# Three stacked attention passes with a routed expert layer: phase two's routing arithmetic on VectorE rewritten, phase three's indirect gathers issued in other slots

## The chip, the cores and the metric

The program runs on one core of one Trainium2 chip. The metric is device time in microseconds from launch to end. A core has five engines that run side by side and meet only at semaphores: TensorE (PE), VectorE (DVE), ScalarE (ACT), GpSimd (POOL) and SyncE (SP), whose queue here only issues transfers.

## The reference

```python
# x: 16 sequences x 256 tokens x 128 features, float32
x = x + layernorm(attention(layernorm(x)))                    # 16 heads, causal
f = layernorm(x)
f = f + attn(ln(f)); f = f + token_moe(ln(f))                 # top 2 of 8 experts, per token
f = f + attn(ln(f)); f = f + seq_moe(ln(f))                   # top 2 of 8, per sequence
x = x + layernorm(f)
...
def _combine_weights(logits):
    vals, idx = jax.lax.top_k(logits, K)
    w = jax.nn.softmax(vals, axis=-1)
    onehot = (idx[..., None] == jnp.arange(E)).astype(w.dtype)
    return jnp.sum(w[..., None] * onehot, axis=-2)
```

## The kernel before

An item is one sequence (256 tokens, two tiles of 128) in one of three attention passes; 16 items make phase one, the next 16 phase two, the last 16 phase three. All queues are written out by hand as a software pipeline. One **step** advances the pipeline by one item and has four **slots**, k = 0 to 3, one for each group of four heads. In step n every engine works on items n-4 to n+2: score maxima of item n, exponentials and values a slot or three behind, the output projection and residual of item n-2, normalisation of item n+2.

The order on each engine is the text of `pe_slot`, `act_slot`, `dve_slot` and `pool_slot`; nothing is reordered, so whatever waits on an engine holds up all that stands behind it there. Landmarks in a step:

- `pe_qk` (L375) opens a step on PE, so its start times count the steps. The maxima (L307, L315) go to one of two PSUM banks, and the next maxima into a bank wait until `dve_reduce` (L616, DVE) has read it. `dve_split_max` (L625) closes a slot's maxima, and `pe_max_T` (L359) waits for it. `pe_o2` (L400) waits for `dve_norm` (L635).
- POOL masks the exponentials (`pool_select`, L902, two a slot), splits q and k into terms (L911, L917), and issues all indirect transfers.

Routing in phase two, for one item: `dve_logits` (L719); `dve_top` piece 0 (top 8 of 8, L731), piece 1 (their indices L736, and the difference of the two best logits, L738, into `gap_all`), piece 2 (L742); a step later `dve_place` piece 0 (one-hots, L754), piece 1 (the sum of the two one-hots, L762, for `pe_rank`, L431 to L435), piece 2 (L765, L769), piece 3 (one-hots times places, two instructions at L773), pieces 4 and 5 (L778, L782). Then `pool_send` scatters the item's rows to DRAM with four indirect transfers (L927).

Between phases two and three the pipeline drains. `dve_tables` turns the counts into tables of jobs in 26 dependent instructions: 18 that the jobs wait for, 8 that phase three needs, the last 3 of them with the exponential of `gap_all` that `act_gap` (L1112) makes. 72 expert jobs of 128 rows follow, their rows loaded from DRAM (L1364, first transposed by PE at L1278), their outputs stored to `y_routed`.

In phase three `pool_fetch` gathers an item's expert outputs with four indirect transfers, pieces 0 to 3 (L946); piece 0 is preceded by a copy of the addresses (L943), whose end POOL waits for. `dve_combine` (L797) adds them: rank 0 in slot 0 once all four have landed, rank 1 in slot 1. The buffer `y_got` is double, by the item's parity. Item n+2 is combined in step n; its four pieces are issued in slots 0 to 3 of step n-1. The last stage, 32 expert passes for the sequence experts, is untouched.

Of the kernel before, what the change touches and what calls it, by code (L numbers as in the profile page):

```python
# [7 lines left out]
ALU = mybir.AluOpType  # L8
# [25 lines left out]
STACK_DMAS = TERMS  # L34
NTOP, NPLACE = 6, 7

# [8 lines left out]
def build(nc, x_in, w_qk, w_v, w_o, b_qk, b_v, b_o, ln1, ln2, gate_w, gate_b, e_w1, e_b1, e_w2, e_b2, out):  # L45
# [13 lines left out]
    with ExitStack() as ctx:  # L59
        def sb(name, shape, dt=F32):  # L60
            return ctx.enter_context(nc.sbuf_tensor(name, shape, dt))
# [86 lines left out]
        lgt = sb("lgt", [P, 2, E])  # L148
        mx = sb("mx", [P, 2, 8])
        mi = sb("mi", [P, 2, 8], U32)  # L150
# [78 lines left out]
        def item(step, d):  # L229
            n, par, phase, lo, hi = step  # L230
            if isinstance(n, int):
                v = n + d
                return Item(v, v % 2, v // B) if lo <= v < hi else None
            return Item(n + d, (par + d) % 2, phase)
# [487 lines left out]
        def dve_top(i, piece):  # L722

            u = i.v - B
            at = NTOP * u
            if piece == 0:
                dve.wait_ge(lg_sb, u + 1)
                need(dve, top, at)
                alone(dve)
                for j in range(2):  # L730
                    nc.vector.max(out=mx[:, j], in_=lgt[:, j]).then_inc(top, 1)  # L731
            elif piece == 1:
                dve.wait_ge(top, at + 2)
                alone(dve)
                for j in range(2):
                    nc.vector.max_index(out=mi[:, j], in_max=mx[:, j], in_values=lgt[:, j]).then_inc(top, 1)  # L736
                gap = gap_all[:, bass.ds(2 * i.b, 2)]
                nc.vector.tensor_tensor(gap, mx[:, :, 1], mx[:, :, 0], ALU.subtract).then_inc(top, 1)  # L738
            else:
                dve.wait_ge(top, at + 4)  # L740
                alone(dve)
                nc.vector.tensor_copy(expert_all[:, bass.ds(2 * i.b, 2)], mi[:, :, 0:TOP]).then_inc(top, 1)  # L742

        def dve_place(i, piece):
# [14 lines left out]
            elif piece == 1:  # L759
                dve.wait_ge(placed, at + 1)  # L760
                need(dve, rank_ps, u)
                nc.vector.tensor_tensor(either[:], onehot[:, :, 0], onehot[:, :, 1], ALU.add).then_inc(placed, 1)  # L762
            elif piece == 2:
# [6 lines left out]
            elif piece == 3:  # L770
                dve.wait_ge(placed, at + 4)
                for t in range(2):
                    m = nc.vector.tensor_tensor(picked[:, t], onehot[:, t],  # L773
                                                places[:, t:t + 1].to_broadcast([P, TOP, E]), ALU.mult)
                m.then_inc(placed, 1)
            elif piece == 4:
# [181 lines left out]
        def pool_slot(step, k):  # L958
# [21 lines left out]
            if k == 3 and nxt and nxt.phase == 2:  # L980
                pool_bias(nxt)
            nxt3 = item(step, 3) if step_phase(step) == 2 else None
            if nxt3:
                pool_fetch(nxt3, k)
            sending = first if k == 3 else item(step, -5)
# [54 lines left out]
        EARLY = [(0, B - 2), (B - 2, B)]  # L1040
        NTABLE_JOBS, NTABLE = 18, 26


        def dve_tables():
# [9 lines left out]
            def view(shape):  # L1054
# [37 lines left out]
                                                op0=ALU.mult, op1=ALU.add))  # L1092
            assert n[0] == NTABLE_JOBS

            t = view([P, NT * TOP, E])
# [14 lines left out]
        def act_gap():  # L1110
            act.wait_ge(top, NTOP * B)
            nc.scalar.activation(gap_all[:], gap_all[:], ACT.Exp).then_inc(gate_a, 1)  # L1112
# [465 lines left out]
        def _(_):  # L1578
# [25 lines left out]

            run_steps(act, behind(act_slot, 0, [loaded, *others]), *RUNS[0])
            act_gap()
            act.wait_ge(table, NTABLE_JOBS)
            pads(act, range(E // 2, E))
            act_jobs()
            act.wait_ge(w1_got, JOBS)  # L1610
# [99 lines left out]
```

## Time and profile before

| | |
|---|---|
| median of three runs | 1174.61 us (1172.34 to 1177.23) |
| profiled execution | 1179.62 us |
| its span | 1177.6 us, mean granted clock 0.961 of full speed |
| PE busy | 1025.1 us, 87% |
| DVE busy | 920.7 us, 78% |
| ACT busy | 780.4 us, 66% |
| POOL busy | 701.0 us, 60% |

Shares of the span mix stages with different limits. By the starts of L375, phases one and two fill the span from 18.7 to about 530 us, the drain and the tables lie between about 530 and 590, the jobs between 590 and 735, phase three between 735 and about 1006, and the sequence experts after it. In a timeline row the columns are start and duration in us, engine, line, operation, output and inputs, shapes and count; the bracket is the idle time of the engine before it and what ended that idle time. A duration begins when the instruction does, so neighbours can overlap and an instruction that waits for a memory port shows the wait in its duration.

### The profile page before, as it was taken

To read this page: it belongs to the slowest core of one execution; us is meant where nothing else is said; L and a number is where in the kernel's file an instruction comes from. 1 tells how busy PE (TensorE), PEld (TensorE's weight loads), DVE (VectorE), ACT (ScalarE), POOL (GpSimd) and SP (SyncE) were. 2 spreads that over 40 slices of the span, in tenths; PEclk is the share of its full clock that TensorE was granted. 3 is DMA by queue.
4 is the path that set the end of the run, shared out by engine and by line. 5 is a ranking of instruction groups with operands and counts; after the bars stand their busy time and mean duration, and the time that the engine had idled before them with its cause. 6 is when DMAs were issued, how large, how long until landed. Compare 5 with 4: busy or idle time off the path is not lost. (4 is left out here: it accounts for less than half of the span.)

```text
span 1177.6 us, 34922 instructions
## 1 busy us (share of the span) xinstructions
PE 1025.1 (87%) x10453; PEld 796.5 (68%) x10453; DVE 920.7 (78%) x2712; ACT 780.4 (66%) x1908; POOL 701.0 (60%) x1034
## 2 busy tenths in 40 slices
PE   1799999999999999998199998288898998989996
PEld 0567676676676766665199998166666665768986
DVE  4679999999989999997647665378898888856675
ACT  1577777777787777775078886167677776755564
POOL 3356666666667888886623332677787786533332
PEclk9999999999999999999589999699999999989999
DMA  5343122221212222221122222244222222100000
GB/s 147 101 113 83 51 56 54 53 56 52 54 51 61 65 66 65 64 68 34 54 62 69 66 70 74 65 126 124 70 63 65 59 65 53 48 2 15 19 19 22
DMA packets 120406, 73.71 MB, mean 63 GB/s; under 512 B 10688, under 2 KB 115264, under 8 KB 120256
## 3 DMA queue, kind: packets, MB, share of 16 engines
q1 hardware_dynamic: 101600, 53.12, 16.5%
q10 hardware_dynamic: 14560, 10.35, 3.2%
q0 software_dynamic: 4096, 8.40, 2.5%
q8 instruction: 76, 1.25, 0.5%
q14 instruction: 74, 0.61, 0.2%
HBM read 21.68 MB, written 11.60 MB: 28 GB/s over the span
## 5 line engine op out<-in xcount | busy, mean ns | idle before, releaser
L616 DVE TENSOR_REDUCE wide<-bank 128x2 f32<-128x512 f32 (+1 forms) x576 | 388.7, 678 | 55.4 <-PE bank L307 40.4
L503 ACT ACTIVATE prob<-bank 128x512 f32<-128x512 f32 x576 | 337.4, 592 | 89.2 <-PE bank L329 58.9
L902 POOL TENSOR_SCALAR_AFFINE_SELECT prob<-prob 128x512 f32<-128x512 f32 x384 | 249.9, 657 | 105.3 <-ACT prob L503 103.4
L348 PE MATMUL bank<-prob,vaug 128*32 128x256 f32 (+1 forms) x3072 | 166.9, 335 | 5.7 <-ACT oT L509 3.2
L1237 POOL COPY w_job<-w_s 128x512 f32 x104 | 67.9, 654 | 154.6 <-PE bank L1206 153.6
L315 PE MATMUL bank<-stack 126*128 126x256 bf16 x768 | 149.8, 276 | 0.0
L334 PE MATMUL bank<-stack 128*128 128x256 bf16 x768 | 148.4, 274 | 1.4 <-ACT prob L503 1.4
L1228 ACT ACTIVATE prob<-bank,b_job 128x128 f32<-128x128 f32 (+1 forms) x416 | 132.5, 400 | 23.7 <-PE bank L1206 12.3
L1217 PE MATMUL bank<-w_job,prob 128*128 128x128 f32 x1088 | 139.7, 276 | 1.9 <-issue 1.8
L348 PEld LDWEIGHTS bank<-prob,vaug 128*32 128x32 f32 x3072 | 81.7, 110 | 80.3 <-issue 48.4
L1217 PEld LDWEIGHTS bank<-w_job,prob 128*128 128x128 f32 x1088 | 132.1, 192 | 4.9 <-issue 3.6
L311 PE MATMUL bank<-maskneg,identb 128*128 128x256 bf16 x384 | 106.6, 278 | 5.5 <-DVE wide L616 4.5
L514 ACT COPY mT<-bank 8x256 bf16<-8x256 bf16 x192 | 68.2, 355 | 45.4 <-PE bank L359 43.3
L329 PE MATMUL bank<-stack 128*128 128x128 bf16 x768 | 75.2, 220 | 15.7 <-DMA stack<-mT 15.1
L927 POOL DMA_INDIRECT x_routed<-hk,x_at x64 | 64.9, 1015 | 37.8 <-DVE x_at L782 18.7
L334 PEld LDWEIGHTS bank<-stack 128*128 128x128 bf16 x768 | 73.9, 98 | 14.3 <-ACT prob L503 3.1
L315 PEld LDWEIGHTS bank<-stack 126*128 126x128 bf16 x768 | 76.5, 100 | 7.0 <-issue 0.5
L625 DVE TENSOR_TENSOR wide<-wide 128x8 bf16<-128x8 f32 x192 | 74.1, 386 | 6.6
L1206 PE MATMUL bank<-oT,w_job 128*128 128x128 f32 x576 | 77.8, 279 | 0.0
L946 POOL DMA_INDIRECT y_got<-y_routed,y_at x64 | 64.4, 1007 | 22.3 <-issue 8.7
L305 PE MATMUL bank<-maskneg,identb 128*128 128x512 bf16 x192 | 74.0, 386 | 4.2 <-DMA stack<-parts 2.2
L307 PEld LDWEIGHTS bank<-stack 126*128 126x128 bf16 x768 | 60.0, 98 | 24.8 <-issue 1.1
(183 smaller groups left out, 2073.1 us busy)
## 6 DMA issues: line engine op xcount, KB each, us to landing
stack<-parts SPq DMA_DIRECT2D x576, 64.0 KB
w_s<-e_w ACTq DMA_DIRECT2D x32, 256.0 KB, 3.0
oT<-x_routed SPq DMA_DIRECT2D x72, 64.0 KB, 1.8
y_routed<-oT SPq DMA_DIRECT2D x36, 128.0 KB, 1.9
stack<-mT SPq DMA_DIRECT2D x192, 4.0 KB
out<-x_all SPq DMA_DIRECT2D x16, 128.0 KB, 1.8
b_all<-e_b ACTq DMA_DIRECT2D x2, 512.0 KB, 8.3
x_routed<-hk,x_at POOLq DMA_INDIRECT x64
```

Of the source, the lines that this page charges most:

```text
L311: nc.tensor.matmul(o[:, :, P:T], identb[:], maskneg[:, 0:2], start=True, stop=False, skip_group_check=True)
L315: m = nc.tensor.matmul(o[:, h], q[:, hh, P:T], k[:, hh, :], start=False, stop=True, skip_group_check=True)
L329: m = nc.tensor.matmul(bk[:, h * P:(h + 1) * P], k[:, p0 + h, P:T], q[:, p0 + h, P:T], start=True, stop=True)
L334: m = nc.tensor.matmul(bk[:, h * T:(h + 1) * T], k[:, hh, 0:P], q[:, hh, :], start=True, stop=True)
L348: m = nc.tensor.matmul(o, w, (prob0, prob1)[kb][:, g % 2, h], start=kb == 0, stop=kb == 1, skip_group_check=True)
L503: nc.scalar.activation(o, s, ACT.Exp, scale=SCALE).then_inc(exp_done, 1)
L616: nc.vector.tensor_reduce(o, s, AX.X, ALU.max, negate=True).then_inc(max_done, 1)
L625: nc.vector.tensor_tensor(upper(g)[:, :, 0], negm[:, g % 2, :, 1], upper(g)[:, :, 1], ALU.subtract).then_inc(negmax, 1)
L902: nc.gpsimd.affine_select(out=t, in_=t, compare_op=ALU.is_ge, fill=0.0, base=0, pattern=[[0, HG], [1, P]], channel_multiplier=-1).then_inc ...
L1206: m = nc.tensor.matmul(bank[2 * par + c // 2][:, (c % 2) * T:(c % 2) * T + width], w1_job[:, par, c * P:(c + 1) * P], rows, start=True, st ...
L1217: m = nc.tensor.matmul(y_bank[par][:, t * P:(t + 1) * P], hid[:, par, c, t * P:(t + 1) * P], w2_job[:, par, c], start=(c == 0), stop=(c == ...
L1228: nc.scalar.activation(hid[:, par, c, 0:width], bank[2 * par + c // 2][:, (c % 2) * T:(c % 2) * T + width], ACT.Gelu, bias=b1_job[:, par, ...
```

## The change

1. The logits' difference (L738) leaves the per-item routing. The top-8 values go to `mx_all`, kept for all tiles, and one instruction in `dve_tables`, the 19th of now 27, takes all differences. `act_gap` waits for it, and moves on ACT from ahead of the four pad transfers to behind them.
2. The two one-hots are joined by a `tensor_reduce` with maximum over the rank axis in place of a `tensor_tensor` addition.
3. One product for both tiles (128x32) in place of two (128x16).
4. In phase three the gathers move. Pieces 0 and 1 of an item go to slot 3 of the step before the one that held them, piece 2 to slot 0, piece 3 to slot 2; slot 1 issues none. The first step issues pieces 0 to 2 of the first item together.

```diff
-NTOP, NPLACE = 6, 7
+NTOP, NPLACE = 5, 7
...
-        mx = sb("mx", [P, 2, 8])
+        mx_all = sb("mx_all", [P, NT, 8])
...
+            mx = mx_all[:, bass.ds(2 * i.b, 2)]
...
-                gap = gap_all[:, bass.ds(2 * i.b, 2)]
-                nc.vector.tensor_tensor(gap, mx[:, :, 1], mx[:, :, 0], ALU.subtract).then_inc(top, 1)
...
-                nc.vector.tensor_tensor(either[:], onehot[:, :, 0], onehot[:, :, 1], ALU.add).then_inc(placed, 1)
+                nc.vector.tensor_reduce(either[:], onehot[:].rearrange("p t r e -> p t e r"), AX.X, ALU.max)\
+                  .then_inc(placed, 1)
...
-                for t in range(2):
-                    m = nc.vector.tensor_tensor(picked[:, t], onehot[:, t],
-                                                places[:, t:t + 1].to_broadcast([P, TOP, E]), ALU.mult)
-                m.then_inc(placed, 1)
+                nc.vector.tensor_tensor(picked[:], onehot[:], places[:].unsqueeze(2).to_broadcast([P, 2, TOP, E]),
+                                        ALU.mult).then_inc(placed, 1)
...
-            nxt3 = item(step, 3) if step_phase(step) == 2 else None
-            if nxt3:
-                pool_fetch(nxt3, k)
+            if step_phase(step) == 2:
+                d, pieces = {0: (3, (2,)), 1: (3, ()), 2: (3, (3,)), 3: (4, (0, 1))}[k]
+                if step[0] == step[3] - 3 and d == 3:
+                    pieces = range(pieces[-1] + 1) if k == 0 else pieces
+                for n in pieces:
+                    if item(step, d):
+                        pool_fetch(item(step, d), n)
...
+            step(nc.vector.tensor_tensor(gap_all[:], mx_all[:, :, 1], mx_all[:, :, 0], ALU.subtract))
...
         def act_gap():
-            act.wait_ge(top, NTOP * B)
+            act.wait_ge(table, NTABLE_JOBS + 1)
...
-            act_gap()
             act.wait_ge(table, NTABLE_JOBS)
             pads(act, range(E // 2, E))
+            act_gap()
```

## Rows read from the trace of the kernel before

**Rows 1.** Windows; busy us of PE, PEld, DVE, ACT, POOL, PEclk, DMA share, GB/s

```profile
350.00:500.00 150.00, 141.79 (x1616) 104.14 (x1614) 143.42 (x455) 113.51 (x259) 120.40 (x166) 1.00 0.24 64
750.00:950.00 200.00, 170.15 (x1823) 119.30 (x1822) 164.31 (x403) 134.51 (x310) 154.94 (x217) 0.96 0.31 84
```

**Rows 2.** Timeline of PE: the first instruction of some steps (L375)

```profile
252.10 1.08 PE L375 MATMUL bank<-xT,wqk_s 128*128 128x256 f32 x4
...
283.12 1.08 PE L375 MATMUL bank<-xT,wqk_s 128*128 128x256 f32 x4
...
346.12 1.08 PE L375 MATMUL bank<-xT,wqk_s 128*128 128x256 f32 x4
...
361.93 1.08 PE L375 MATMUL bank<-xT,wqk_s 128*128 128x256 f32 x4
...
514.42 1.08 PE L375 MATMUL bank<-xT,wqk_s 128*128 128x256 f32 x4
...
758.93 1.89 PE L375 MATMUL bank<-xT,wqk_s 128*128 128x256 f32 x4
...
881.66 1.08 PE L375 MATMUL bank<-xT,wqk_s 128*128 128x256 f32 x4
...
898.63 1.13 PE L375 MATMUL bank<-xT,wqk_s 128*128 128x256 f32 x4
...
1006.41 1.08 PE L375 MATMUL bank<-xT,wqk_s 128*128 128x256 f32 x4
```

**Rows 3.** Timeline of DVE in one step of phase two

```profile
395.12 0.46 DVE L738 TENSOR_TENSOR gap_all<-mx 128x2 f32<-128x2 f32 x1
395.50 0.68 DVE L616 TENSOR_REDUCE wide<-bank 128x2 f32<-128x512 f32 x1
...
399.80 0.61 DVE L762 TENSOR_TENSOR either<-onehot 128x16 bf16<-128x16 f32 x1
400.84 0.69 DVE L616 TENSOR_REDUCE wide<-bank 128x4 f32<-128x512 f32 x1 [0.43 <-PE bank L307]
...
401.90 1.14 DVE L679 TENSOR_TENSOR f_all<-f_all,att 128x256 f32<-128x256 f32 x1
...
410.70 0.56 DVE L773 TENSOR_TENSOR picked<-onehot,places 128x16 f32<-128x16 f32 x2
```

**Rows 4.** Instructions by tile; ns min/median/max, first and last start

```profile
L754 DVE TENSOR_TENSOR onehot<-expert_all,iota_e x16: 181/669/677, 348.3 to 569.6; 128x32 f32<-128x32 f32 x16
L762 DVE TENSOR_TENSOR either<-onehot x16: 160/612/614, 349.3 to 569.8; 128x16 bf16<-128x16 f32 x16
...
L778 DVE TENSOR_REDUCE place_all<-picked x16: 178/180/186, 362.3 to 571.1; 128x4 f32<-128x32 f32 x16
```

**Rows 5.** Timeline of PE in the same step of phase two: two waits for DVE

```profile
397.95 0.44 PE L400 MATMUL bank<-ident,on 128*128 128x128 f32 x2 [0.35 <-DVE on L635]
...
404.89 0.29 PE L359 MATMUL bank<-identb,wide 128*128 128x128 bf16 x2 [0.28 <-DVE wide L625]
```

**Rows 6.** Timeline of DVE and PE where the jobs begin

```profile
587.80 0.22 DVE L1245 COPY b_job<-b_all 128x128 f32 x1
...
590.29 0.45 PE L1278 MATMUL bank<-ident,oT 128*128 128x128 f32 x1 [19.94 <-DMA oT<-x_routed]
```

**Rows 7.** Who waited for the gathers (L946): us, times

```profile
  DVE f_all L797: 30.2, 16
```

**Rows 8.** Timeline of POOL, DVE and PE around one combine of phase three

```profile
842.24 1.11 POOL L946 DMA_INDIRECT y_got<-y_routed,y_at  x1 [0.17 <-issue]
...
845.44 0.98 POOL L946 DMA_INDIRECT y_got<-y_routed,y_at  x1 [0.16 <-issue]
...
849.21 0.61 DVE L797 SCALAR_TENSOR_TENSOR f_all<-y_got,weight_all,f_all 128x128 f32<-128x128 f32 x2 [2.42 <-DMA y_got<-y_routed,y_at]
...
849.83 0.97 POOL L946 DMA_INDIRECT y_got<-y_routed,y_at  x1 [0.82 <-ACT prob L503]
...
852.12 0.27 PE L359 MATMUL bank<-identb,wide 128*128 128x128 bf16 x2 [2.98 <-issue]
```

More of the change, by code:

```diff
@@ L1040, in build @@
         EARLY = [(0, B - 2), (B - 2, B)]
-        NTABLE_JOBS, NTABLE = 18, 26
+        NTABLE_JOBS, NTABLE = 18, 27
         def dve_tables():
```

## The prediction

> **What bounds the kernel now.** I read the windows by stage first, because the change touches two stages that need not have the same limit. In phase two PE is busy 141.79 of 150 us and DVE 143.42 at the full clock: both are nearly full, and DVE is the fuller one. In phase three PE is busy 170.15 and DVE 164.31 of 200, so neither is full and something makes both wait; the granted clock there averages 0.96 [rows 1]. The starts of L375 on PE then give the length of a step. Phase one: (283.12 - 252.10) / 2 = 15.51 us. Phase two, once all of the routing and the scatters run: (514.42 - 361.93) / 9 = 16.94; the one step in which the routing's DVE work is already there but the scatters are not, 346.12 to 361.93, takes 15.81. Phase three: (1006.41 - 758.93) / 14 = 17.68, while a step in it that goes well, 881.66 to 898.63, takes 16.97 [rows 2]. The waits say why. In phase two PE waits 0.35 us at L400 and 0.28 at L359 for DVE [rows 5]. In phase three DVE waits for the gathers in all 16 items, 30.2 us together [rows 7], and in the worst steps PE then stands still for 2.98 us at L359, for which DVE should have finished its maxima [rows 8].
>
> **Phase two: the difference, L738, removed.** It starts at 395.12 and the next instruction at 395.50: it costs DVE 0.38 us a step, in a stretch with no idle time, ahead of the normalisation that L400 waits for [rows 3]. All of this is worth having.
>
> **The two products made one.** The pair takes 0.56 us [rows 3]. The trace has no 128x32 product, but L754 has that shape, two inputs in SBUF and one result: 0.181 at its shortest, 0.669 in the median [rows 4]. So the new instruction saves between 0.56 - 0.18 = 0.38 and nothing. The first of the old pair passes quickly and the second is held, which speaks for the low price; I take 0.2 us saved. This too lies ahead of L400.
>
> **The one-hots joined by a maximum.** The addition takes 0.612 in the median and 0.160 at its shortest; a reduction of as many inputs, L778, takes 0.178 to 0.186 in all its 16 executions [rows 4]. So DVE gains 0.61 - 0.18 = 0.43. But right behind it DVE already idles 0.43 us until PE's L307 [rows 3], so this gain only lengthens that idle time, and I count nothing; at worst (a result as slow as the old one) it costs nothing either.
> L762 is 0.61 or 0.16 with the same shape, while L778 never varies. The Trainium skill (SBUF — State Buffer, Who interferes with whom) says that a `tensor_tensor` with both inputs in SBUF contends with a GpSimd instruction that reads SBUF, and that a `tensor_reduce` on trn2 never does; the trace agrees. By that rule L762 becomes 0.18. A sentence of the same page (SBUF: two separate sides) speaks against it: reads that go to a new 16-byte line each time pay a penalty, and the new reduction steps 32 bytes between its two inputs; no run here shows that penalty. By neither does the sum move, since the idle time behind takes both.
>
> **What DVE's relief is worth.** DVE saves 0.38 + 0.2 = 0.58 us a step on the loop through L400. PE can give back no more than the difference to the step that ran undisturbed, 16.94 - 15.81 = 1.13, and no less than its wait of 0.35 at L400 [rows 2, 5]. The 0.28 at L359 comes after L679, which takes 1.14 us [rows 3] and is untouched; it stays unless POOL's work happens to shift. I take 0.57 us: the 0.35 and a little over a quarter of the other 0.78, in waits too small to have rows. Nine full steps are measured and two more run before the drain: 11 x 0.57 = 6.3 us, with ends 9 x 0.35 = 3.2 and 11 x 1.13 = 12.4.
>
> **The tables.** One more dependent instruction, about 0.2 us (the shortest two-input ones, rows 4), stands behind the 18 that the jobs wait for. DVE's preparations end at 587.80 + 0.22 = 588.02 and PE's first job instruction starts at 590.29, waiting for a load that comes from instruction 18 by way of SP [rows 6]. So 2.27 us cover it: nothing; without cover 0.2 us. `act_gap` moves behind four transfers on ACT's queue; its reader is DVE's instruction 25, and what it is late by, up to 2 us, has the same cover. What is queued behind it on ACT waits for the same load as PE. Nothing again.
>
> **Phase three: the gathers moved.** POOL still issues four gathers and one copy per item; SP's queue is not touched. Take the worst step. Piece 3 is issued at 845.44 and takes POOL 0.98; DVE starts its combine at 849.21, so the landing takes 849.21 - 846.42 = 2.79 us after that. DVE was ready at 849.21 - 2.42 = 846.79 [rows 8]. In the new order the last piece goes where piece 2 stood, 842.24 to 843.35; with the same 2.79 it lands at 846.14, still 0.65 before DVE is ready. On average DVE waits 30.2 / 16 = 1.9 us [rows 7], so the usual case has more room. The wait goes in every step. The new first pieces are a whole step ahead of their combine and need the item two before it to be combined, which happened two slots earlier on DVE.
> What remains is a step without this stall. It can't be shorter than phase one's 15.51, which has about the same matmuls on PE; and 881.66 to 898.63 shows 16.97 where PE did not wait for the combine in slot 0, with all other waits still in it. The order itself helps those: the copy of addresses and the 0.82 us that POOL waits behind it [rows 8] leave slot 0, where they stood ahead of the q/k split. On the other side DVE's second combine in slot 1 still meets POOL's masks. I take the middle, (15.51 + 16.97) / 2 = 16.24: 14 x (17.68 - 16.24) = 20.2 us. Ends: 14 x 0.71 = 9.9 and 14 x 2.17 = 30.4. The first step of the phase issues the same pieces in nearly the same order: about nothing.
>
> **Sum.** 6.3 + 20.2 = 26.5 us. From the profiled execution's 1179.62: 1153.1. That execution lies 5.0 above the median of the runs, 1174.61, so for the median I say 1148.
>
> **Rivals.**
> *Only the stall goes.* Steps of phase three fall to 16.97 because DVE and POOL go on blocking each other at L797 and the masks, and phase two gives only the wait at L400: 9.9 + 3.2 = 13.1, 1161.5. For it: in phase three DVE and POOL are both above 77% busy [rows 1] and that step was measured. Against it: POOL's slot 0 gets lighter. Chance 0.20.
> *Both stages reach their floors.* 12.4 + 30.4 = 42.8, 1132. It needs L679 to meet POOL in another phase and no contention at all. Chance 0.08.
> *The stall is the transfer's, not the issue's.* If landing were held by something that ends at a fixed point of the step, earlier issue would not help; only phase two's 6.3 would remain: 1168.3. Against it: landing after issue varies, but the worst is 2.79 us. Chance 0.04.
> *POOL piles up in slot 3: slower.* Ahead of slot 0's first mask stood one gather, 0.16 + 0.98 = 1.14 us; now stand a copy of about 0.2, 0.82 of waiting, and two gathers of 0.97 with 0.16 between: 3.1. The masks of slot 0 come 2.0 us later, and the values (L348) on PE need them in slot 1. Against it: POOL is busy 154.94 of 200 us [rows 1], so about 4 us of each step are waits that can take it up. If all 2.0 were uncovered it would cost 28 us and more than undo the 26.5: 1176 as it stands, and over 1180.5 if the masks are 2.4 us late. It decides from 1.9 us uncovered. Chance 0.05, of which 0.03 beyond 0.5%.
>
> **How the numbers follow.** The forecast has 0.63. 0.5% of 1174.6 is 5.9 us, about what a measurement of this kernel can tell from no change. Faster by more (below 1168.7): 0.63 + 0.20 + 0.08 + half of the transfer rival, 0.92. Within: 0.05. Slower: 0.03. The range reaches from 1136 (a good part of the way to the floors) to 1162 (only the stall goes); what lies outside is the extreme of the floors and the last two rivals, and the outer parts of the second.
>
> **What the new profile would show.** L946 no longer releases DVE: its wait at L797 falls from 30.2 us to near nothing, but for the first item. Steps of phase three by L375: 16.0 to 16.5, with few waits of PE over 1 us at L359. L762 a reduction of 0.18; L738 once, at the tables. Steps of phase two: 16.3 to 16.5, with no wait at L400 and a longer idle time of DVE before L307. First job instruction on PE as far behind the drain as before. I am wrong if the masks of slot 0 (L902) now hold L348, or if steps in phase three stay at 17 because L311 waits for DVE behind the second combine.

## The result and the profile after

The changed kernel takes 1156.79 us in the median of 4 runs (1155.36 to 1158.09), the kernel before 1173.79 on the same chip. The ratio is 0.9851, with a 95% interval of 0.9824 to 0.9877: 17.0 us faster. The forecast was 1148 with a range of 1136 to 1162, so the sign and the range held, and the gain is 9 us short of the point.

First the windows over the two stretches of [rows 1].

```profile
350.00:500.00 150.00, 140.44 (x1629) 105.66 (x1650) 138.91 (x442) 113.20 (x262) 121.66 (x169) 1.00 0.24 65
750.00:950.00 200.00, 179.51 (x1966) 130.26 (x1994) 170.45 (x434) 143.42 (x334) 164.17 (x233) 0.97 0.32 88
```

In phase two PE is as busy as before (140.44 of 150 us against 141.79) while DVE has fallen by 4.5 us: there DVE got lighter, and PE went hardly faster. In phase three every engine does more in the same 200 us, at nearly the same clock (0.97 against 0.96): waits have gone. The starts of L375 on PE, as in [rows 2], say how much:

```profile
344.12 1.08 PE L375 MATMUL bank<-xT,wqk_s 128*128 128x256 f32 x4
...
359.93 1.08 PE L375 MATMUL bank<-xT,wqk_s 128*128 128x256 f32 x4
...
510.53 1.08 PE L375 MATMUL bank<-xT,wqk_s 128*128 128x256 f32 x4
...
754.36 1.17 PE L375 MATMUL bank<-xT,wqk_s 128*128 128x256 f32 x2
...
837.69 1.08 PE L375 MATMUL bank<-xT,wqk_s 128*128 128x256 f32 x4
...
853.89 1.08 PE L375 MATMUL bank<-xT,wqk_s 128*128 128x256 f32 x4
...
984.36 0.87 PE L375 MATMUL bank<-xT,wqk_s 128*128 128x256 f32 x3
```

The step without scatters takes 359.93 - 344.12 = 15.81 us, to the hundredth what it took before. A full step of phase two takes (510.53 - 359.93) / 9 = 16.73 (before 16.94). A step of phase three takes (984.36 - 754.36) / 14 = 16.43 (before 17.68), and the usual one 853.89 - 837.69 = 16.20. The spans, 1156.4 against 1177.6, differ by 21.2 us: 14 steps of phase three give 17.5, nine of phase two 1.9, and the way from 510.53 to the first job 2.3. Another 2.0 stem from ahead of 346.12, in code that the change doesn't touch; the jobs, the start of phase three and the tail took 1.1, 0.6 and 0.9 more.

Who waited for the gathers (L944), as in [rows 7]:

```profile
  DVE f_all L795: 12.9, 2
```

It is 12.9 us in two waits, where it was 30.2 in 16. Both belong to the first two items (10.69 us at the first, 2.25 at the second). The timeline of DVE shows the first of them, and one of the later combines, which have no wait:

```profile
736.13 1.32 DVE L795 SCALAR_TENSOR_TENSOR f_all<-y_got,weight_all,f_all 128x128 f32<-128x128 f32 x4 [10.69 <-DMA y_got<-y_routed,y_at]
...
839.86 0.62 DVE L795 SCALAR_TENSOR_TENSOR f_all<-y_got,weight_all,f_all 128x128 f32<-128x128 f32 x2
```

The first two items waited nearly as long in the kernel before:

```profile
741.65 1.31 DVE L797 SCALAR_TENSOR_TENSOR f_all<-y_got,weight_all,f_all 128x128 f32<-128x128 f32 x4 [9.93 <-DMA y_got<-y_routed,y_at]
...
749.50 1.26 DVE L797 SCALAR_TENSOR_TENSOR f_all<-y_got,weight_all,f_all 128x128 f32<-128x128 f32 x4 [3.59 <-DMA y_got<-y_routed,y_at]
```

So 13.5 of the 30.2 us were no part of the steady steps. The other 14 items waited 0.51 to 2.42 us, 16.7 together, and it is these waits that went.

The new instructions by tile, as in [rows 4] (ns: shortest, median, longest; first and last start):

```profile
L761 DVE TENSOR_REDUCE either<-onehot x16: 175/188/190, 347.3 to 564.3; 128x16 bf16<-128x32 f32 x16
L772 DVE TENSOR_TENSOR picked<-onehot,places x16: 173/486/522, 357.7 to 565.3; 128x32 f32<-128x32 f32 x16
```

The maximum never takes over 0.19 us, as foreseen. The single product takes 0.49 in the median, hardly less than the pair's 0.56.

### The profile page after: what moved, and what is told of

It reads as the page before. It is cut to its first block, busy times and chain, and to the rows that moved or that the text cites. A ratio compares the mean times of both kernels' runs of the same rounds, so it can differ in the third digit from the quotient of the medians.

```text
span 1156.4 us, 34796 instructions
## 1 busy us (share of the span) xinstructions
PE 1007.1 (87%) x10358; PEld 794.4 (69%) x10453; DVE 891.7 (77%) x2681; ACT 772.8 (67%) x1908; POOL 695.3 (60%) x1034
## 4 chain that ended last, share of the span: by engine, by line
PE 31%; DVE 5%; issue 5%; DMA 3%; POOL 3%; ACT 2%; SPq 1%; POOLq 0%; DVEq 0%; ACTq 0%
PE bank L1220 10%; PE bank L1209 10%; PE bank L348 2%; DMA stack<-mT 2%; DVE wide L616 2%; PE bank L393 1%; POOL y_got L944 1%; PE bank L315 1%; PE bank L334 1%; PE bank L375 1%; PE bank L311 1%; PE bank L1281 1%; DVE f_all L795 1%; PE bank L329 1%; PE bank L381 1%
## 5 line engine op out<-in xcount | busy, mean ns | idle before, releaser
L348 PE MATMUL bank<-prob,vaug 128*32 128x256 f32 (+1 forms) x3072 | 165.6, 333 | 7.5 <-issue 3.8
L1240 POOL COPY w_job<-w_s 128x512 f32 x104 | 64.3, 619 | 158.3 <-PE bank L1209 157.1
L348 PEld LDWEIGHTS bank<-prob,vaug 128*32 128x32 f32 x3072 | 81.5, 109 | 81.4 <-issue 49.4
L307 PE MATMUL bank<-stack 126*128 126x128 bf16 x768 | 75.0, 219 | 15.7 <-ACT prob L503 6.4
L944 POOL DMA_INDIRECT y_got<-y_routed,y_at x64 | 63.9, 998 | 24.7 <-POOL y_at L941 13.1
L625 DVE TENSOR_TENSOR wide<-wide 128x8 bf16<-128x8 f32 x192 | 69.8, 364 | 6.6
```

What stands on the lines that cost most here:

```text
L307: m = nc.tensor.matmul(o[:, h], q[:, p0 + h, 0:P], k[:, p0 + h, 0:P], start=False, stop=True, skip_group_check=True)
L348: m = nc.tensor.matmul(o, w, (prob0, prob1)[kb][:, g % 2, h], start=kb == 0, stop=kb == 1, skip_group_check=True)
```

## Where phase two's gain went

The same step of phase two in the timelines, first of the kernel before, three lines of PE, ACT and POOL that were not among the rows ahead of the prediction; its next L375 follows at 412.79:

```profile
395.85 1.08 PE L375 MATMUL bank<-xT,wqk_s 128*128 128x256 f32 x4
...
398.97 0.60 ACT L503 ACTIVATE prob<-bank 128x512 f32<-128x512 f32 x1
...
401.59 1.17 POOL L911 TENSOR_TENSOR rest<-qkf,parts 128x512 f32<-128x512 f32 x1
```

And after the change, lines of PE, ACT, POOL and DVE from the step that starts at 393.40:

```profile
395.01 0.44 PE L400 MATMUL bank<-ident,on 128*128 128x128 f32 x2
...
396.35 0.58 ACT L503 ACTIVATE prob<-bank 128x512 f32<-128x512 f32 x1
...
397.88 1.00 POOL L925 DMA_INDIRECT x_routed<-hk,x_at  x1 [0.16 <-issue]
...
397.90 0.69 DVE L616 TENSOR_REDUCE wide<-bank 128x4 f32<-128x512 f32 x1 [0.86 <-PE bank L307]
...
398.92 1.17 POOL L909 TENSOR_TENSOR rest<-qkf,parts 128x512 f32<-128x512 f32 x1
...
398.96 1.42 DVE L679 TENSOR_TENSOR f_all<-f_all,att 128x256 f32<-128x256 f32 x1
```

By "held" this text means that a DVE instruction takes longer than at its shortest while a GpSimd instruction runs beside it; L679 at its shortest takes 0.42 us, in the step from 344.12 for one. The "split" is GpSimd's first subtraction of the q/k terms, L911 before and L909 after. Count from the start of the step. L400 stands at 1.61 instead of 2.10, with no wait: PE is 0.49 us earlier, and DVE idles 0.86 before the reduction instead of 0.43. So far all is as forecast. But ScalarE's exponential starts at 2.95 instead of 3.12, only 0.17 earlier, since it stands behind ScalarE's own queue. GpSimd's mask, scatter and q/k split follow it in order, and the split starts at 5.52 instead of 5.74. L679 on DVE started earlier, but is held until after the split has ended: 1.42 us instead of 1.14. It ends at 6.98 instead of 7.19. The step got shorter by exactly this 0.21.

Over all nine steps from 359.93 the rest of the step, from the end of L679 on, takes 9.75 us (9.74 to 9.76), and in the kernel before as well (9.75, once 9.79). In these steps the length is L679's end plus a constant. It is not so in the step from 344.12, which has no scatters: there L679 ends at 5.89 and 9.92 follows, so with an end as early as that something else sets the step. The experiments test the constant below.

## Experiments

**The two halves apart.** First the kernel before with only the new order of the gathers:

```
-            nxt3 = item(step, 3) if step_phase(step) == 2 else None
-            if nxt3:
-                pool_fetch(nxt3, k)
+            if step_phase(step) == 2:
+                d, pieces = {0: (3, (2,)), 1: (3, ()), 2: (3, (3,)), 3: (4, (0, 1))}[k]
...
```

> The kernel before with the gathers of phase three moved and the routing as it was. If the gain is mostly the stall at the combine, steps of phase three fall from 17.68 to about 16.4 us as in the changed kernel, steps of phase two stay at 16.94, and the time is about 1160 to 1161 us (a ratio to before of 0.989). If instead the gathers' order gives little and the routing most, it stays above 1168 (0.995).

Measured: 1160.09 us, ratio 0.9851 (0.9809 to 0.9893). Steps of phase three take 16.37, those of phase two 16.93. The waits for the gathers in its trace:

```profile
  DVE f_all L797: 12.4, 2
```

Then the changed kernel with the old order of the gathers (the same lines the other way round).

> The changed kernel with the gathers back in slots 0 to 3. Phase two's steps as in the changed kernel, 16.73 us, phase three's as before. Theory: 2 us in the steps and 2 in the drain, so 1169 to 1171 us (0.996 to 0.998). Rival, the routing is worth the 6.3 us that I had forecast: 1167.5 or less (0.9946). The two edits should add up to the whole within 2 us.

Measured: 1175.55 us, ratio 0.9982 (0.9959 to 1.0005). Steps of phase two take 16.74, those of phase three 17.59, with two of about 20 us (20.41 and 19.70) as in the kernel before (19.75 and 20.26). The waits for the gathers:

```profile
  DVE f_all L795: 30.9, 15
```

What follows: the new order of the gathers alone gives the whole of what the run times can show, and without it the stall is there as before. The routing by itself can't be told from no change by run times: its interval reaches from 4.8 us faster to 0.6 slower. Its 0.2 us a step is read from the step lengths.

**The routing's three edits, one at a time.** Each was taken back in the changed kernel. The difference once per item:

```
                     nc.vector.max_index(out=mi[:, j], in_max=mx[:, j], in_values=lgt[:, j]).then_inc(top, 1)
+                gap = gap_all[:, bass.ds(2 * i.b, 2)]
+                nc.vector.tensor_tensor(gap, mx[:, :, 1], mx[:, :, 0], ALU.subtract).then_inc(top, 1)
...
-            step(nc.vector.tensor_tensor(gap_all[:], mx_all[:, :, 1], mx_all[:, :, 0], ALU.subtract))
...
-            act.wait_ge(table, NTABLE_JOBS + 1)
+            act.wait_ge(top, NTOP * B)
```

> The changed kernel with the logits' difference back in each item, its maximum and its one product kept. Read by steps of phase two. If this difference (0.38 us of VectorE ahead of L400) is what shortened the step, steps go back from 16.73 to about 16.9, the wait of PE at L400 comes back, about 0.3 us. If the other two edits carry it, steps stay at 16.73 to 16.75.

Measured: one run at 1160.57; steps of phase two 16.90 (six of nine between 16.90 and 16.92). Its step from 394.46, timelines of PE and DVE:

```profile
396.53 0.44 PE L400 MATMUL bank<-ident,on 128*128 128x128 f32 x2 [0.33 <-DVE on L635]
...
400.49 1.13 DVE L679 TENSOR_TENSOR f_all<-f_all,att 128x256 f32<-128x256 f32 x1
```

L400 waits 0.33 us again, the split is back at 5.69, L679 ends at 7.16 and the step is 16.90: of the 0.21 the difference carries 0.17.

The addition in place of the maximum:

```
-                nc.vector.tensor_reduce(either[:], onehot[:].rearrange("p t r e -> p t e r"), AX.X, ALU.max)\
-                  .then_inc(placed, 1)
+                nc.vector.tensor_tensor(either[:], onehot[:, :, 0], onehot[:, :, 1], ALU.add).then_inc(placed, 1)
```

> The changed kernel with the addition in place of the maximum. VectorE idles 0.86 us behind the maximum, so the 0.43 us that the addition costs more should only shorten that: steps of phase two stay at 16.73 us, the idle time before L616 falls to about 0.43. Rival, it lay on the path: steps of 17.0 or more.

Measured: one run at 1156.06; steps of phase two 16.73. By tile, its addition:

```profile
L761 DVE TENSOR_TENSOR either<-onehot x16: 162/172/611, 347.4 to 564.5; 128x16 bf16<-128x16 f32 x16
```

Once the rest had moved, the same addition that took 0.61 before took 0.17: in its step from 393.56 it starts at 397.01, between two masks of GpSimd (396.19 to 396.83 and from 397.25), while in the kernel before it started at 399.80 beside a mask from 399.73 to 400.38. The duration belonged to the place, not to the operation.

The two products in place of one:

```
-                nc.vector.tensor_tensor(picked[:], onehot[:], places[:].unsqueeze(2).to_broadcast([P, 2, TOP, E]),
-                                        ALU.mult).then_inc(placed, 1)
+                for t in range(2):
+                    m = nc.vector.tensor_tensor(picked[:, t], onehot[:, t],
+                                                places[:, t:t + 1].to_broadcast([P, TOP, E]), ALU.mult)
+                m.then_inc(placed, 1)
```

> The changed kernel with the two products of 128x16. Forecast of the prediction: 0.2 us of VectorE. The new single product took 0.49 us where the pair took 0.56, so it should be about 0.07 us and steps stay at 16.73 to 16.80.

Measured: one run at 1157.63; steps of phase two 16.73. The pair takes 0.55 us again and L679 1.36 instead of 1.42: it starts 0.06 later and ends at the same 6.98.

**L679 one place later on DVE.** This is the first attempt to get past the hold: the residual sum behind the next reduction of maxima.

```
-            if i.phase > 0:
-                dve.wait_ge(res, base + 1)
+
+        def dve_residual_sum(i):
+            if i.phase == 1:
+                dve.wait_ge(res, NRES * i.v + 1)
                 nc.vector.tensor_tensor(pair(f_all, i), pair(f_all, i), att[:, i.par], ALU.add).then_inc(res, 1)
...
+                dve_residual_sum(older)
                 dve_residual_stats(older)
```

> The changed kernel with the residual's second addition (L679) put behind the next reduction of maxima in phase two. Moving the scatter showed that L679 is held by whichever GpSimd instruction lies beside it. Port theory: here it meets only the last 0.6 us of the split, the reductions of slot 1 come 0.4 to 1.3 us earlier, PE's wait at L359 in slot 2 (0.27) goes, and steps of phase two fall from 16.73 to about 16.3: 4 to 5 us less than the changed kernel. Rival, the values or the scatter on GpSimd bound the step: it stays at 16.7.

Measured: 1156.25 us, ratio 0.9844 (0.9809 to 0.9878); steps of phase two 16.67. The expected 16.3 did not come. Its step from 393.15, DVE and PE:

```profile
399.25 0.88 DVE L681 TENSOR_TENSOR f_all<-f_all,att 128x256 f32<-128x256 f32 x1
...
401.92 0.28 PE L359 MATMUL bank<-identb,wide 128*128 128x128 bf16 x2 [0.62 <-DVE wide L625]
```

The sum now takes 0.88, but it still ends at 399.25 + 0.88 - 393.15 = 6.98, with the split; the 0.28 us that PE waited at L359 became 0.62. A later place for the held instruction gives only 0.06 us a step (9.69 instead of 9.75 behind its end), since the split ends when it did.

**The scatter of slot 0 moved.** So the split itself has to come earlier. Ahead of it stands slot 0's scatter. Three places for it were tried. The first was slot 1:

```
-                pool_send(sending, (k + 1) % NG)
+                for n in {3: (0,), 0: (), 1: (1, 2), 2: (3,)}[k]:
+                    pool_send(sending, n)
```

> The changed kernel with phase two's scatter of slot 0 issued in slot 1, behind the split of q and k, so that slot 1 issues two and slot 0 none. Port theory: GpSimd's first split (L909) then runs about 1.0 us earlier in the step, is over before the residual's second addition (L679) comes, L679 falls from 1.42 to about 0.45 us, a step of phase two from 16.73 to 15.8 to 16.0 us, and the time by 8 to 10 us to about 1148. Rival, ScalarE's exponential holds PE at L307 (the trace charges 0.54 us a step to it): L679 may get shorter but steps stay at 16.7 and the time at 1157.

Measured: 1162.82 us, ratio 0.9875 (0.9839 to 0.9911); steps of phase two 17.13. The expectation of 15.8 to 16.0 was wrong. Its step from 392.27, POOL and DVE:

```profile
396.73 1.16 POOL L909 TENSOR_TENSOR rest<-qkf,parts 128x512 f32<-128x512 f32 x1
...
398.04 0.85 DVE L679 TENSOR_TENSOR f_all<-f_all,att 128x256 f32<-128x256 f32 x1
...
404.64 0.91 DVE L662 TENSOR_SCALAR hn<-f_all,post_mv,post_r 128x128 f32<-128x128 f32 x2 [0.63 <-POOL post_r L893]
```

The split came at 4.46 and L679 ended at 6.62, 0.36 earlier (held by GpSimd's mask behind the split). But the second scatter in slot 1 pushed back the standard deviations that GpSimd computes behind it, and DVE then waited for them for 0.63 us: the part behind L679 grew from 9.75 to 10.55.

Slot 2 was tried together with another order of the gathers (one a slot, pieces 0, 1, 2, 3 in slots 3, 0, 1, 2):

```
-                pool_send(sending, (k + 1) % NG)
+                for n in {3: (0,), 0: (), 1: (1,), 2: (2, 3)}[k]:
+                    pool_send(sending, n)
...
-                d, pieces = {0: (3, (2,)), 1: (3, ()), 2: (3, (3,)), 3: (4, (0, 1))}[k]
...
+                d, pieces = {0: (3, (1,)), 1: (3, (2,)), 2: (3, (3,)), 3: (4, (0,))}[k]
...
```

> Again one edit in each phase. Phase two: the scatters as 1, 0, 1, 2 alone, the addition where it was. It should meet slot 1's first mask (0.64 us) instead of the split (1.17): L679 about 0.85 us, steps 16.4 to 16.6. Phase three: the gathers one a slot, each one slot earlier than before the change (piece 0 in slot 3, 1, 2, 3 in slots 0, 1, 2), copy kept. If only the landing of the last piece matters, the wait at the combine is gone here too and steps are 16.2 to 16.4, as in the changed kernel; if the free slot 1 matters as well, they stay near 16.9, the length of the steps before that did not stall.

Measured: 1162.04 us, ratio 0.9881 (0.9854 to 0.9908); steps of phase two 17.08, of phase three 16.55. In phase two, DVE and PE:

```profile
399.64 0.42 DVE L679 TENSOR_TENSOR f_all<-f_all,att 128x256 f32<-128x256 f32 x1
...
411.41 0.92 PE L375 MATMUL bank<-xT,wqk_s 128*128 128x256 f32 x3 [1.27 <-ACT xT L602]
```

Here L679 is not held at all: 0.42 us. Yet PE waits 1.27 at the start of the next step, for the transposed input that ScalarE brings late, and the part behind L679 takes 11.35 in this step and 11.07 in the usual one. Phase three has no wait for gathers from the third item on (12.0 us, twice), and its steps are still 0.12 longer than the changed kernel's. Two effects nearly cancel in that tenth: in the usual step the split starts at 5.50 instead of 5.76 to 5.80, but the gather in slot 1 stands behind it, and from the end of GpSimd's second subtraction, L915, to the next L375 it is 7.50 us instead of 7.10.

The third place was slot 3, behind piece 0, where GpSimd waits anyway:

```
-                pool_send(sending, (k + 1) % NG)
+                for n in {3: (0, 1), 0: (), 1: (2,), 2: (3,)}[k]:
+                    pool_send(sending, n)
```

> The changed kernel with slot 0's scatter (piece 1) issued in slot 3 of the step before, right behind piece 0; nothing else differs. It takes the scatter away from ahead of the q/k split L909 without burdening slots 1 and 2, where a second scatter cost 0.4 us a step. In the changed kernel's step from 393.40 the first scatter starts at 394.69 and takes 0.97, the copy 0.40 and the two masks 0.64 and 0.63, then comes the scatter of 1.00 and the split. With both scatters in front (1.26 us more, with the 0.30 between two issues) the masks run at 397.3 and 397.9 and the split starts at 398.6 instead of 398.92. Theory (the end of the split holds L679, and L679 sets the rest of phase two's step): L679 is released 0.3 us earlier, the step falls by 0.2 to 0.3 to 16.45 to 16.55, 11 steps give 2 to 3 us. Rival (GpSimd's masks in order behind the scatters set the pace, whatever L679 takes): the first mask of slot 0 comes 1.26 us later and slot 1's values wait for it; the step lengthens to 17.0 to 17.2, as in the two kernels that had two scatters in one slot. Phase three 16.2 to 16.5 by both.

Measured: 1155.38 us, ratio 0.9818 (0.9784 to 0.9852). Steps of phase two take 16.44, as the theory said. Two of its steps, by PE, POOL and DVE:

```profile
395.30 0.87 PE L375 MATMUL bank<-xT,wqk_s 128*128 128x256 f32 x3
...
400.04 1.15 POOL L909 TENSOR_TENSOR rest<-qkf,parts 128x512 f32<-128x512 f32 x1
...
400.77 1.30 DVE L679 TENSOR_TENSOR f_all<-f_all,att 128x256 f32<-128x256 f32 x1
...
401.16 0.63 POOL L900 TENSOR_SCALAR_AFFINE_SELECT prob<-prob 128x512 f32<-128x512 f32 x1
...
461.38 1.08 PE L375 MATMUL bank<-xT,wqk_s 128*128 128x256 f32 x4
...
466.13 1.16 POOL L909 TENSOR_TENSOR rest<-qkf,parts 128x512 f32<-128x512 f32 x1
...
466.85 0.72 DVE L679 TENSOR_TENSOR f_all<-f_all,att 128x256 f32<-128x256 f32 x1
...
467.25 0.83 POOL L900 TENSOR_SCALAR_AFFINE_SELECT prob<-prob 128x512 f32<-128x512 f32 x1
...
477.32 1.08 PE L375 MATMUL bank<-xT,wqk_s 128*128 128x256 f32 x4
```

In both the split starts 4.74 or 4.75 behind the step's start and L679 at 5.47, and in both GpSimd's mask comes right behind the split. In the first the mask takes 0.63 us and L679 is held on until 0.28 behind the mask, 6.77; the step is 16.52. In the second L679 is free 0.28 behind the split, at 6.19, and it is the mask that takes longer, 0.83; the step is 15.94. Four steps go the first way and this one the second; what decides is not shown. In two more, from 477.32 and 493.64, the split starts later, at 5.14, yet L679 ends at 6.58 and 6.57, and the step is 16.32. So the step follows L679's end, and neither the start of the split nor the end of the mask (6.49, 6.70 and 7.07). The rest behind L679 is 9.74 to 9.76 in eight of the nine steps. It is the same in the kernel before, in the changed one and in all seven experiments that leave L679 in its place and put no second scatter in slot 1 or 2 (this one included), all but for one step in each of three, from an end at 6.19 to one at 7.24.

**The gathers' addresses without the copy.** The new order leaves a copy of the addresses on GpSimd and a wait of 0.82 us for it. Here the gathers read the whole table:

```
-                nc.gpsimd.tensor_copy(y_at[:, i.par], y_at_all[:, bass.ds(2 * i.b, 2)]).then_inc(fetch_at, 1)
-                pool.wait_ge(fetch_at, u + 1)
-                alone(pool)
...
-                bass.IndirectOffsetOnAxis(ap=y_at[:, i.par, t, rank:rank + 1], axis=0))\
+                bass.IndirectOffsetOnAxis(ap=y_at_all[:, 2 * i.b + t, rank:rank + 1], axis=0))\
```

> The changed kernel with the gathers' addresses read straight from the table for all tiles, without the copy and the 0.81 us that GpSimd waits behind it. If GpSimd is what is late in phase three (the masks of slot 0 end at the moment when the split of the maxima wants the port, and the mask of slot 1 holds the values for 0.32 us), its work ends 1.0 us earlier, the waits of PE at L348 (0.32) and at L359 (0.15) go, and steps fall from 16.20 to about 15.8: 5 to 6 us, about 1151. If phase three is held by PE and the transfers of mT, nothing over 1 us is gained.

Measured: 1157.01 us, ratio 0.9821 (0.9785 to 0.9858); steps of phase three 16.44, not the expected 15.8. Its step from 852.67, POOL and DVE:

```profile
854.84 1.25 DVE L795 SCALAR_TENSOR_TENSOR f_all<-y_got,weight_all,f_all 128x128 f32<-128x128 f32 x2
...
856.94 0.63 POOL L900 TENSOR_SCALAR_AFFINE_SELECT prob<-prob 128x512 f32<-128x512 f32 x1 [1.00 <-ACT prob L503]
```

GpSimd was early and then waited 1.00 us for ScalarE's exponential, while its first mask (855.28, 0.66 us) now stood beside DVE's combine, which took 1.25 us instead of 0.62. The split started at 6.02 instead of 5.78.

**All of it together.** Scatters as in the kernel with two in slot 2, L679 later, no copy, and three gathers in slot 3:

```
-                d, pieces = {0: (3, (2,)), 1: (3, ()), 2: (3, (3,)), 3: (4, (0, 1))}[k]
...
+                d, pieces = {0: (3, ()), 1: (3, ()), 2: (3, (3,)), 3: (4, (0, 1, 2))}[k]
...
```

> Two edits on the changed kernel that lie in different phases, so that each is read from its own steps. Phase two: scatters of slots 3, 0, 1, 2 go from 1, 1, 1, 1 to 1, 0, 1, 2, and the residual's second addition stands behind the next reduction. The split of q and k then ends before that addition and the scatter no longer delays the division's operands in slot 1: steps from 16.73 to 16.1 to 16.4 us if GpSimd's place in slots 0 and 1 is what holds the step; 17 or more if two scatters in slot 2 make slot 3's masks late. Phase three: no address copy, three gathers in slot 3, none in slot 0, so that the split follows slot 0's second mask directly, 0.8 us earlier: PE's wait of 0.33 us at L348 goes and steps fall from 16.2 to 15.9; if they stay at 16.2 to 16.4, not the split's place but the transfer of mT and VectorE hold them. Both together 8 to 14 us less than the changed kernel.

Measured: 1170.63 us, ratio 0.9947 (0.9926 to 0.9968): this lost two thirds of the gain. Steps of phase two take 17.18, of phase three 17.10. Phase three, from 842.54, POOL and PE:

```profile
846.46 1.23 POOL L903 TENSOR_SCALAR_AFFINE_SELECT prob<-prob 128x512 f32<-128x512 f32 x2
...
849.25 0.86 PE L348 MATMUL bank<-prob,vaug 128*32 128x256 f32 x16
```

The masks behind three gathers start at 3.92 in the step and PE's values in slot 1 at 6.71; in the changed kernel they stand at 3.41 and 6.08. That is the rival in which GpSimd piles up in slot 3. The other edits leave this phase alone or were run without it: the scatters and L679's place belong to phase two, and without the third gather the steps are 16.44 (no copy alone) and 16.17 (the next experiment). So the third gather in slot 3 costs 0.7 to 0.9 us a step. In phase two this kernel differs from the one with two scatters in slot 2 only by the later L679, and takes 0.10 more (17.18 against 17.08).

**The two harmless edits together.** L679 later and no copy; neither alone gave a gain in time that can be measured.

> The changed kernel with both small edits that cost nothing by themselves: the residual sum behind the next reduction of maxima (alone: steps of phase two 16.67, 1156.25), and the gathers' addresses read from the whole table, without the copy and the 0.8 us wait behind it (alone: 16.44 in phase three, 1157.01). Theory (each edit only moves a hold to another instruction): phase two 16.67, phase three 16.35 to 16.45, the whole 1154 to 1157, within 0.3% of the changed kernel. Rival (two freed places add up, since L679's hold and the copy's wait both delay the q/k split): phase three falls to 16.1 or less, the whole to 1150 or less.

Measured: 1154.37 us, ratio 0.9817 (0.9788 to 0.9846). Steps of phase two take 16.67, as expected; those of phase three 16.17, between the theory's 16.35 and the rival's 16.1, and nearer the rival. Four steps of its trace take 15.88, three 16.32 or 16.33. One of each, POOL, from 867.34 (15.88) and from 883.22 (16.32):

```profile
871.03 0.63 POOL L903 TENSOR_SCALAR_AFFINE_SELECT prob<-prob 128x512 f32<-128x512 f32 x1 [0.44 <-ACT prob L503]
...
872.78 1.17 POOL L912 TENSOR_TENSOR rest<-qkf,parts 128x512 f32<-128x512 f32 x1
...
887.49 0.63 POOL L903 TENSOR_SCALAR_AFFINE_SELECT prob<-prob 128x512 f32<-128x512 f32 x1 [1.02 <-ACT prob L503]
...
889.25 1.17 POOL L912 TENSOR_TENSOR rest<-qkf,parts 128x512 f32<-128x512 f32 x1
```

Split at 5.44, step 15.88; split at 6.03, step 16.32. Where GpSimd waits 0.44 for the exponential the step is good, where it waits 1.02 it is not. But the pair of edits is not what made the good steps. L679's new place is an edit of phase two, and in phase three this kernel runs the same instructions in the same order as the one without the copy, whose steps from the sixth on all have the late split (6.02 to 6.10) and take 16.32 to 16.52. So the same queues can settle into different patterns, and no run shows what decides. The 16.17 is therefore one trace's and no proof of the rival, and the freed copy is worth something only in the pattern in which ScalarE's exponential comes in time.

The ratios of this kernel, of the one with two scatters in slot 3 and of the one without the copy (0.9817, 0.9818, 0.9821) lie some 0.3% below the changed kernel's 0.9851, but the intervals overlap (0.9788 to 0.9846 against 0.9824 to 0.9877 for the first), and the third has no shorter steps. The runs don't settle it; what is shown is the shorter steps of phase two with two scatters in slot 3.

## Why the prediction was right, and where it expected too much

**The stall at the combine: right.** It went from every step behind the first two items, and the split experiment shows that the order of the gathers does it alone. The waits went once the pieces were issued earlier, so the rival of a transfer held elsewhere falls. The average wait was misread: 30.2 / 16 = 1.9 us takes in the first two items, which had 13.5 and keep 12.9. The other 14 waited 1.2 us on average.

**What remains of a step of phase three: nearly right.** The guess was the middle between 15.51 and 16.97, 16.24; the usual step is 16.20. A middle has no mechanism, so that it came within 0.04 is luck; that the step would fall below 16.97 was argued, with the lighter slot 0. The mean is 16.43, because the first steps of the phase take longer (17.78 the first, 16.76 the fourth; the kernel before had 16.98 and 17.41 there) and one more, the tenth, takes 16.73 in this trace and within 0.02 of it in most others. So 17.5 us came instead of 20.2. What holds the usual step is GpSimd's order, in the timelines of POOL and PE:

```profile
843.47 1.17 POOL L909 TENSOR_TENSOR rest<-qkf,parts 128x512 f32<-128x512 f32 x1
...
845.47 1.32 POOL L915 TENSOR_TENSOR parts<-rest,parts 128x512 bf16<-128x512 f32 x1 [0.25 <-ACT parts L562]
...
846.74 0.63 POOL L900 TENSOR_SCALAR_AFFINE_SELECT prob<-prob 128x512 f32<-128x512 f32 x1
...
847.48 0.86 PE L348 MATMUL bank<-prob,vaug 128*32 128x256 f32 x16 [0.32 <-issue]
```

The two subtractions of the q/k split and the masks beside them follow each other with 0.25 us of waiting, and the values (L348) start 0.11 us behind the end of the last mask. The next L375 starts 7.09 to 7.12 us behind the end of L915 in ten kernels, from the fifth step of the phase to the last but one, whether the step takes 15.88, 16.20 or 16.73. In the three that issue a gather in slot 1, the kernel before among them, it is 7.4 at the least and mostly 7.5 or more. That takes the fall from 16.97 to 16.20 apart: L915 ends 0.36 earlier, as the lighter slot 0 promised, and 0.41 less follows, which goes with the empty slot 1 and which the prediction had not priced. GpSimd is busy 82% of the stage (164.17 of 200 us) and still on the path.

**Phase two: the mechanism right, its worth too high.** The step that failed is the worth of DVE's relief: "no less than its wait of 0.35 at L400", and "I take 0.57 us" a step. The wait went, and PE was 0.49 earlier at that place, but the step only got 0.21 shorter, less than the lower end. The prediction had written that L679 "is untouched" and that the 0.28 at L359 behind it "stays unless POOL's work happens to shift", and had not asked what ends L679. It ends with GpSimd's split, whose place is set by ScalarE and GpSimd, two engines that DVE's relief doesn't reach. The steps came to 16.73, outside the 16.3 to 16.5 that it named for the new profile. Nine steps gave 1.9 us and the stretch from 510.53 to the first job 2.3, where 6.3 was said for eleven steps. That stretch takes 73.3 to 74.2 us in the kernels with the new routing that have no second scatter in slot 1 or 2, 74.8 with the difference back in each item, and 75.2 and 75.9 in the two with the old routing; two steps of 0.21 explain 0.4 of it, the rest was not taken apart. Of the three edits the removed difference carries 0.17 of the 0.21; for the product 0.2 us was taken, its row gives 0.07 and its step nothing; the maximum lay under idle time, as foreseen.

The Trainium skill (SBUF — State Buffer, Who interferes with whom) says that a DVE instruction with two SBUF inputs contends with a GpSimd instruction that reads SBUF and that a reduction on trn2 never does. By that rule the maximum stays short, and so the trace has it (0.175 to 0.190 in all 16); and L679 is held by the split, which is what the experiments turned on. The prediction used the rule for the instruction that was changed and not for the one behind it.

**The tables: right that they cost nothing, though by a thin margin.** The timelines of DVE and PE, as in [rows 6]:

```profile
580.29 0.18 DVE L1108 TENSOR_SCALAR weight_all<-gap_all 128x32 f32<-128x32 f32 x1 [1.39 <-ACT gap_all L1115]
...
584.07 0.45 PE L1281 MATMUL bank<-ident,oT 128*128 128x128 f32 x1 [19.25 <-DMA oT<-x_routed]
```

DVE now waits 1.39 us for the exponential that was moved behind four transfers (up to 2 was said), its preparations end at 584.47, and PE had started at 584.07. The cover of 2.27 us is used up; the first job was not late for it, since its own wait ends with the load.

**The median.** Of the 9 us that the point lies too low, 5 are the sum's: 1153.1 was said for the profiled execution and 1158.09 came. The rest is the step from execution to median: 5.0 us was taken off because the profiled execution before lay that much over its median, while the one after lies 1.3 over. A slip that changes nothing: the prediction's chances of a gain beyond 0.5% add up to 0.93, not 0.92.

## What to carry to other kernels

When a step is held by a chain that passes through several engines, price a relief by following it to the end of the step: at each instruction ask what ended it. An engine queue that runs in order beside the relieved one can take back most of it within the same step, even below the size of the wait that went. Search the trace for an instruction whose end lies a constant time before the end of every step; here it was found after the fact, but the trace of the kernel before has it in all nine steps of phase two. The constant holds only while that instruction is the late one, as the step from 344.12 and the two kernels with a second scatter in slot 1 or 2 show. And one trace of a loop can sit in one of several patterns, so a step length that only one trace shows is weak evidence for a small edit. And a consumer that stalls for a transfer is helped by an earlier place in the issuing queue, as long as that place has idle time: with two gathers in slot 3 the steps got shorter, a third made them 0.7 to 0.9 us longer.

## What the runs showed that was not expected

- One and the same addition (128x16) takes 0.61 us in the kernel before and 0.17 in the changed one with the addition put back; only its place relative to GpSimd's work differs.
- The end of a held DVE instruction follows that of GpSimd's: L679 ends 0.28 or 0.29 us behind the split whether it starts 0.04 us behind the split's start (1.42 long) or 0.57 behind it (0.88 long). Starting earlier gains nothing.
- With a mask right behind the split, L679 can be free after the split (0.72 long, and the mask takes 0.83 instead of 0.63) or only after the mask (1.30 long), at starts that differ by 0.01 us. In the kernel with two scatters in slot 3 this made the step 15.94 or 16.52.
- An indirect DMA costs GpSimd 0.94 to 1.23 us per issue, and 0.30 us lie between two in a row, besides the way to the landing (2.3 us in the median for the scatters). A second one in slot 1 or 2 cost the step 0.40 and 0.35 us; in slot 3 it gained 0.29.
